# A recurrent layer with low-rank weights padded to full tiles, and VectorE's first scans moved ahead of the group sum

## The reference, cut to what matters

```python
xa = _ln(x, ln1_w, ln1_b)
sx = concatenate([state[:, 1:2] - xa[:, :1], xa[:, :-1] - xa[:, 1:]], axis=1)
xxx = tanh((xa + sx * maa_x) @ maa_w1).reshape(b, l, 5, DM)          # DM = 32
xxx = einsum('blfd,fde->blfe', xxx, maa_w2)
xm = xa[:, :, None] + sx[:, :, None] * (maa_stack + xxx)
xk, xw, xv, xr, xg = (xm[:, :, j] for j in range(5))
w = exp(-exp(time_decay + tanh(xw @ td_w1) @ td_w2))                 # td_w1: 256 x 64
r, k, v = xr @ Wr.T, xk @ Wk.T, xv @ Wv.T;  g = silu(xg @ Wg.T)
def step(s, rkvw):                                                   # along the sequence
    a = k_t[..., :, None] * v_t[..., None, :]
    out = einsum('bhi,bhij->bhj', r_t, u * a + s)
    return a + w_t[..., :, None] * s, out
og = group_norm(out) * gn_w + gn_b                                   # per head of 8
x1 = x + og * g @ Wo.T
# then a second row norm and a small feed-forward, added to x1
```

## Time and profile before

| | us |
|---|---|
| median of three runs | 963.16 (961.91 to 963.85) |
| profiled execution | 962.38 |
| its span, first to last instruction | 960.6 |
| TensorE busy | 918.6 (96%) |
| VectorE busy | 591.4 (62%) |
| ScalarE busy | 462.9 (48%) |
| GpSimd busy | 413.3 (43%) |

### The profile page before, as it was taken

The page is one execution under the profiler, slowest core; times in us unless marked ns, Lnnn a source line. Parts: engine busy times, 40 slices in busy tenths (PEclk is TensorE's granted clock), DMA queues, the critical chain, the costliest instruction groups (busy, mean ns, idle before and its releaser), DMA issues.

```text
span 960.6 us, 23348 instructions
## 1 busy us (share of the span) xinstructions
PE 918.6 (96%) x9345; PEld 767.8 (80%) x9345; DVE 591.4 (62%) x974; ACT 462.9 (48%) x1026; POOL 413.3 (43%) x572
## 2 busy tenths in 40 slices
PE   6999989988999999999999999999998999899998
PEld 4777767976778889888887888888887888678775
DVE  5899986776654343544356443344436757998883
ACT  3677775237743433333435333333333344566565
POOL 2143345965346443423256443343323952343231
PEclk9999999999999999999999999999999999999999
DMA  9100000410011101112101110111100100000000
GB/s 295 47 23 2 2 1 2 140 56 1 2 56 51 53 26 44 53 51 56 56 8 56 51 56 25 55 40 56 51 24 18 56 1 1 2 1 7 12 7 23
DMA packets 24177, 37.64 MB, mean 39 GB/s; under 512 B 4432, under 2 KB 16528, under 8 KB 23824
## 3 DMA queue, kind: packets, MB, share of 16 engines
q1 hardware_dynamic: 24080, 36.23, 12.2%
HBM read 35.17 MB, written 1.05 MB: 38 GB/s over the span
## 4 chain that ended last, share of the span: by engine, by line
PE 70%; DVE 14%; ACT 6%; POOL 5%; issue 5%; DMA 0%; SPq 0%; DVEq 0%; ACTq 0%; POOLq 0%
PE ps L1299 18%; PE ps L790 13%; PE ps L1316 10%; PE ps L1957 6%; PE ps L1334 4%; PE ps L890 3%; PE ps L1360 3%; PE ps L1344 2%; DVE sb L2485 2%; DVE sb L656 1%; DVE sb L650 1%; PE ps L2035 1%; PE ps L421 1%; PE ps L270 1%; PE ps L2121 1%
## 5 line engine op out<-in xcount | busy, mean ns | idle before, releaser
L837 POOL TENSOR_TENSOR sb<-sb 128x256 fp32r<-128x256 f32 (+1 forms) x128 | 102.0, 797 | 255.3 <-DMA sb<-in_heads_a 135.3
L1299 PE MATMUL ps<-sb 128*128 128x512 f32 x768 | 188.4, 395 | 1.0 <-issue 1.0
L1299 PEld LDWEIGHTS ps<-sb 128*128 128x128 f32 x768 | 139.5, 188 | 33.7 <-issue 6.1
L790 PE MATMUL ps<-sb 128*128 128x256 f32 x1152 | 148.8, 286 | 0.2 <-DVE sb L936 0.2
L790 PEld LDWEIGHTS ps<-sb 128*128 128x128 f32 x1152 | 141.5, 191 | 2.6 <-issue 0.6
L839 POOL TENSOR_TENSOR sb<-sb 128x256 fp32r<-128x256 f32 (+1 forms) x128 | 118.4, 925 | 10.0
L1511 DVE TENSOR_REDUCE sb<-ps 128x8 f32<-128x520 f32 x32 | 22.4, 700 | 126.3 <-PE ps L1334 126.3
L1316 PE MATMUL ps<-sb 128*128 128x256 f32 x768 | 99.1, 285 | 0.4 <-DVE sb L1499 0.4
L1316 PEld LDWEIGHTS ps<-sb 128*128 128x128 f32 x768 | 95.0, 191 | 3.0 <-issue 0.9
L1434 ACT ACTIVATE sb<-ps,sb 128x512 f32<-128x512 f32 x64 | 43.8, 685 | 107.4 <-PE ps L1299 107.4
L1531 DVE SCALAR_TENSOR_TENSOR sb<-ps,sb 128x512 fp32r<-128x512 f32 x64 | 45.1, 746 | 72.1 <-ACT sb L1467 72.1
(11 more groups left out here) (221 smaller groups left out, 1674.5 us busy)
## 6 DMA issues: line engine op xcount, KB each, us to landing
sb<-in_heads_a SPq DMA_DIRECT2D x32, 386.0 KB, 3.1
sb<-in_heads_c SPq DMA_DIRECT2D x16, 256.0 KB, 3.8
sb<-in_heads_b SPq DMA_DIRECT2D x32, 128.0 KB, 3.2
sb<-in_mlp_a SPq DMA_DIRECT2D x16, 128.5 KB, 2.0
sb<-in_mlp_b SPq DMA_DIRECT2D x16, 128.0 KB, 2.1
sb<-in_w_r SPq DMA_DIRECT2D x1, 2048.0 KB, 7.6
sb<-in_encT SPq DMA_DIRECT2D x1, 1024.0 KB, 6.4
sb<-in_ctx SPq DMA_DIRECT2D x1, 1024.0 KB, 8.3
```

The lines of the kernel that those rows point to most:

```text
L790: last = pe.matmul(m.acc(t), lhsT[x], rhs[w], start=opens and n == 0, stop=False, skip_group_check=True)
L837: pool.tensor_tensor(high, src, one, ALU.mult).then_inc(*G.did(name + "_high", u))
L1299: last = pe.matmul(m.ps[u][:, c, :], m.w_parts[u][w][:, (KD * q + k) * P:(KD * q + k + 1) * P], rows[x][:, k, c * 512:(c + 1) * 512], star ...
```

## The change

Two things are changed. The low-rank weights are padded with zeros: the lora weight from five blocks of 64 columns to six, so that its third product has 128 columns too; the first decay weight from 64 to 128 columns and the second from 64 to 128 rows, with ScalarE's tanh between them over 128 partitions. And in VectorE's slot `scan0` is called behind `products1` and ahead of `group_sum`, where it stood behind `lora_rows` before; in the drain the two are swapped in the same way.

```diff
--- before.py
+++ after.py
@@ -36,7 +36,7 @@
 HS = 8
 DM, ND = 32, 5
 DD = 64
-NX = 5 * 64
+NX = 6 * 64
 
 COLS = [("ln1_s", 2), ("ln1_b", 2), ("bq_self", 2), ("bk_self", 2), ("bv_self", 2), ("ln2_s", 2), ("ln2_b", 2),
         ("bq_cross", 2), ("bk_cross", 2), ("bv_cross", 2), ("ln3_s", 2), ("ln3_b", 2),
@@ -1978,10 +1978,9 @@
         pe.wait_ge(*m.own_vec.at("xl", i))
         if i >= 1:
             pe.wait_ge(*done["mixed"].at(i - 1))
-        for n, width in enumerate((P, P, 2 * DM)):
-            cols = slice(n * P, n * P + width)
-            last = product(m.mx_ps[0:width, n * P:(n + 1) * P],
-                           [(m.maa_w1[:, k, cols], m.xl[i % 2][:, k, :]) for k in range(KD)])
+        for n in range(NX // P):
+            cols = slice(n * P, (n + 1) * P)
+            last = product(m.mx_ps[:, cols], [(m.maa_w1[:, k, cols], m.xl[i % 2][:, k, :]) for k in range(KD)])
         last.then_inc(*done["lora"].did(i))
 
     @of_tile
@@ -2004,7 +2003,7 @@
             pe.wait_ge(m.s_acc, 16)
         if i >= 1:
             pe.wait_ge(*done["ew"].at(i - 1))
-        product(m.td_ps[0:DD, 0:P], [(m.td_w1[:, k, :], mixed(i, MIX_W, k)) for k in range(KD)])\
+        product(m.td_ps[:, 0:P], [(m.td_w1[:, k, :], mixed(i, MIX_W, k)) for k in range(KD)])\
             .then_inc(*done["td1"].did(i))
 
     @of_tile
@@ -2226,7 +2225,7 @@
         act.wait_ge(*done["td1"].at(i))
         if i >= 1:
             act.wait_ge(*done["td2"].at(i - 1))
-        act.activation(m.td[:, :], m.td_ps[0:DD, 0:P], ACT.Tanh).then_inc(*done["td"].did(i))
+        act.activation(m.td[:, :], m.td_ps[:, 0:P], ACT.Tanh).then_inc(*done["td"].did(i))
 
     @of_tile
     def gate(i):
@@ -2572,12 +2571,12 @@
             vec.wait_ge(m.s_biased, 5)
             add_half(vec, m, 1)
         products1(slot - 5)
+        scan0(slot - 5)
         group_sum(slot - 6)
         shift(slot - 3)
         lora_rows(slot - 3)
         if slot == 3:
             mlp_split(vec, ph, m, 1, 1, 3)
-        scan0(slot - 5)
         group_rstd(slot - 6)
         group_norm(slot - 6)
         scan1(slot - 5)
@@ -2594,8 +2593,8 @@
     bonus(LAST - 1)
     out_heads(LAST - 1)
     products1(LAST)
+    scan0(LAST)
     group_sum(LAST - 1)
-    scan0(LAST)
     group_rstd(LAST - 1)
     group_norm(LAST - 1)
     scan1(LAST)
@@ -2735,13 +2734,13 @@
             {"self": sb([P, S])[:, :], "cross": sb([P, TILES * S])[:, :]} for _ in range(2))
 
         m.s0 = m.mask_mul["cross"][:, 0:TILES * HS * 4].rearrange("p (t n) -> p t n", t=TILES)
-        m.td_w2 = m.mask_mul["cross"][0:DD, TILES * HS * 4:TILES * HS * 4 + D]
+        m.td_w2 = m.mask_mul["cross"][:, TILES * HS * 4:TILES * HS * 4 + D]
         for masks in (m.mask_mul, m.mask_add):
             masks["cross"] = masks["cross"].rearrange("p (t s) -> p t s", s=S)
 
         m.maa_w1, m.maa_w2 = sb([P, KD, NX]), sb([P, 3, D])
         m.sel, m.gather, m.center = sb([P, 2, P]), sb([P, 2, 32]), sb([P, P])
-        m.td_w1 = sb([P, KD, DD])
+        m.td_w1 = sb([P, KD, P])
         m.vj = 3
 
         m.wa, m.wb = pair([P, PACK_A]), pair([P, D])
@@ -2827,7 +2826,7 @@
         m.av, m.sc = cut(0, at, [HS, 4, S]), cut(0, at, [HS, D])
         m.th, m.ew = cut(0, at, [D]), cut(0, at, [D])
         at = [rest]
-        m.td, m.og, m.sq, m.tok, m.yT = cut(1, at, [P], DD), cut(1, at, [D]), cut(1, at, [D]), cut(1, at, [D]), cut(1, at, [KD, P])
+        m.td, m.og, m.sq, m.tok, m.yT = cut(1, at, [P]), cut(1, at, [D]), cut(1, at, [D]), cut(1, at, [D]), cut(1, at, [KD, P])
         m.xc = cut(1, at, [KD, 2, S + 1])
         m.kr, m.kk, m.thf, m.rf = (cut(1, at, [D]) for _ in range(4))
 
@@ -3057,8 +3056,8 @@
     p, n = np.arange(P)[:, None], np.arange(P)[None, :]
     same = p // HS == n // HS
     turned = n % 16 == p // HS
-    w1 = np.zeros((KD, P, ND, 2 * DM), np.float32)
-    w1[:, :, :, 0:DM] = L3("maa_w1").reshape(KD, P, ND, DM)
+    w1 = np.zeros((KD, P, NX // (2 * DM), 2 * DM), np.float32)
+    w1[:, :, 0:ND, 0:DM] = L3("maa_w1").reshape(KD, P, ND, DM)
     w2 = np.zeros((2, 2 * DM, 3, D), np.float32)
     for f in range(ND):
         w2[f % 2, 0:DM, f // 2], w2[f % 2, DM, f // 2] = L3("maa_w2")[f], L3("maa_stack").reshape(ND, D)[f]
@@ -3078,7 +3077,8 @@
         "w_qkv": block(L0("w_qkv")), "w_ao": block(L0("w_ao")), "w_q": block(L0("w_q")), "w_kv": block(L0("w_kv")),
         "w_co": block(L0("w_co")),
         "w1x1": np.ascontiguousarray(np.stack([L1(n) for n in ("Wn", "Wm", "Wl", "Wo")]).transpose(2, 0, 1)),
-        "maa_w2": w2.reshape(P, 3, D), "maa_w1": w1.reshape(KD, P, NX).transpose(1, 0, 2), "td_w1": block(L3("td_w1")), "td_w2": L3("td_w2"),
+        "maa_w2": w2.reshape(P, 3, D), "maa_w1": w1.reshape(KD, P, NX).transpose(1, 0, 2), "td_w1": np.pad(block(L3("td_w1")), ((0, 0), (0, 0), (0, P - DD))),
+        "td_w2": np.pad(L3("td_w2"), ((0, P - DD), (0, 0))),
         "w_r": np.ascontiguousarray(np.stack(stack).transpose(2, 0, 1).reshape(KD, P, 8, D).transpose(1, 2, 0, 3)),
         "s0": np.ascontiguousarray(ctx[:, 2:2 + HS, :].reshape(TILES, 2, KD, P, HS).transpose(3, 0, 4, 2, 1)
                                    [:, :, values].reshape(P, TILES, HS * 4)),
```

## The result

| | before | after |
|---|---|---|
| median, us | 961.92 (14 runs, 959.25 to 963.85) | 966.51 (14 runs, 963.38 to 967.39) |
| ratio, 95% interval | | 1.0047 (1.0037 to 1.0057) |
| span of the profiled execution | 960.6 | 965.3 |

The change makes the kernel 0.47% slower. 963.8 was forecast, and the result lies above the range. The forecast added 0.6 us to the 963.16 of three runs; against the 961.92 of fourteen the change costs 4.6 us.

The account below looks back on a forecast made before the run. VectorE was taken to bound the first stretch, TensorE the second, a chain of latencies the drain. Terms -0.2 + 1.0 + 1.4 - 2.2 + 0.6 = +0.6 on 963.16 gave 963.8 us; range 960.3 to 966.2.

Parts of the forecast that it names:

- second stretch: 850.3 to 923.9 us, TensorE sets the pace: padding saves 0.61 a round for three rounds, 0.33 in the fourth; -2.2 us.
- 0.18 of cover: In later rounds, TensorE's 18.14 us was to stay longer than VectorE's 17.96, so that TensorE sets the round.
- Entry: Start of the layer: first two lora products save 0.25 and 0.14, scans cost +0.29, shorter first stall -0.1; net -0.2 us.
- First stretch: 803.4 to 850.3 us, VectorE sets the pace: late group norm costs +1.0 us in its first round, +1.4 in the second.
- Drain: Last tiles at the layer's end: later group sum delays the root and GpSimd's gate product; +0.6 us.
- the slower one: Rival: VectorE becomes the bound in later rounds, 18.7 us or more each; +2.8 us, 966.0; chance 0.22.
- The faster one: Rival: VectorE's shift does not stand behind GpSimd's operation, so both stalls go; -3.7 us, 959.5; chance 0.23.
- the padding saves nothing: Rival: wider weight loads show between TensorE's passes; +0.4 us at the layer's start, 2.2 not regained, 966.4; chance 0.08.

## Why the prediction was wrong

The step that failed is the second stretch, and in it the sentence that the saving "needs a TensorE round of 18.14 to be the longest, against VectorE's 17.96: 0.18 of cover". Both sums were right to 0.1: TensorE's is 18.14 with the padding alone, and VectorE's is 18.93 - 0.88 = 18.05 in the changed kernel. But the longest of two engines' sums is not the round. The loop over both is a third candidate, and it is longer than either. The rows for it were there: before, `turn_ffn` came 0.95 behind `ffn`'s end, of which some 0.15 is the hand-over (889.14 to 889.29 after), so 0.80 was in hand. From `mix1` to `ffn` VectorE grew from 13.93 to 15.10, by 1.17, and the padded TensorE reaches `turn_ffn` 0.42 sooner after `mix1` (868.44 to 883.32 with the padding alone, 14.88; 870.28 to 885.58 before, 15.30). 1.17 + 0.42 - 0.80 = 0.79, the 18.93 less 18.14 that was measured. With the growth of 0.87 that the prediction itself had for VectorE, the loop would have come out at 18.63, and most of the saving would have been gone. By size, the second stretch is 2.75 us of the 4.1 by which the change in span (4.7) differs from the forecast (0.6), the first stretch 0.96 and the drain 0.35.

Term by term:
- **Entry**, -0.2: -0.16 at the second `mix2`, and -0.03 at the bonus product behind the first round's scans (820.32 against 820.35), where the forecast has its -0.2. In this run the layer itself begins 0.28 later (its first `shift` at 786.46 against 786.18), so the change's own gain is 0.31 there. The term was right to about 0.1.
- **First stretch**, +1.0 and +1.4: +3.36. The mechanism was right, the size was not: the shift takes 1.95 (about 1.9 forecast), the turn of the heads waits 1.73 (1.5 forecast). Each round lacked the scans' wait of 0.31 for the product ahead of them, which group sum, shift and lora rows had hidden; with it the turn of the heads is 1.53 + 0.31 = 1.84 late, which is what the trace has (829.40 against 827.56). The -0.2 that the sum took over from the entry was not there, as just said. The sum itself, 1.53 - 0.2 - 0.45, makes 0.88 and not 0.83; nothing hangs on that.
- **Second stretch**, -2.2: +0.55. The 1.17 are the shift's stall (+1.53), the first of the five scans that no longer stands (-1.15), the scans' wait (+0.31) and the last scan beside GpSimd's gate product (+0.46), together 1.15. The stall and the gate product were in the forecast for VectorE's sum; the wait was not, and none of them was set against `ffn`. Of the -2.2, 0.33 was for the fourth round, which lies in the last piece. It does not come even with the padding alone (46.23 against 46.24): there TensorE waited for `ffn` already before.

```profile
921.91 0.41 PE L2098 MATMUL ps<-sb 128*128 128x128 f32 x2 [0.60 <-DVE sb L2546]
```

- **Drain**, +0.6: +0.95. The wait for GpSimd is 1.20, as forecast; the scans' wait of 0.31 is about the rest by size, but that was not tried by itself.

Of the rivals, the slower one named the right stretch and nearly the right time (966.0), but not the cause: VectorE kept 0.88 of idle time a round, and with `ffn` earlier the same work fits into 18.14. The faster one is refuted by the shift itself. That the padding saves nothing is refuted by the padding alone, at 0.61 a round.

By the Trainium skill (TensorE: Matmul & The Clock Gate, LDWEIGHTS) a load takes its time by its columns, so the wider loads, with nothing hidden, would have given back some of the saving. Here they gave back nothing: the 0.61 is what the prediction had worked out without them, and TensorE's passes fill 54.43 of 54.43 while the loads are busy for 45.52 of the same time. The Trainium skill (SBUF — State Buffer, Who interferes with whom) has VectorE contend with a GpSimd operation that reads SBUF when it has two inputs in SBUF itself, and never in a reduction. The trace agrees: beside GpSimd's 1.81 the two-input shift took 1.95, the group sum 0.39.

## What to carry to other kernels

Where a stretch is near balance between two engines, the longest engine sum is not enough: follow each buffer that one engine hands back to the other, and add up the whole way round. An instruction that waits with time in hand shows how far such a loop is from setting the pace; subtract from that both what the waited-for engine loses and what the waiting one gains. An edit that shortens the waiting engine's way to the wait spends the same slack as one that delays the other, and what it saves past that is lost: here the padding is worth 0.61 a round with the old order and 0.18 with the new one.

An instruction between a result and its first reader can hide the hand-over, even on one and the same engine (here 0.31 a round). Before it is moved away, ask what it covered.

## What the runs showed of the hardware that was not expected

- VectorE can wait for its own results: 0.23 us of idle time between the 1.20 us product and the scans that read it, in every round but the first where the scans stand right behind it. With the group sum between them there is none of it, and the group sum itself starts 1.12 behind the product's start, the scans alone 1.43. Not every such hand-over costs as much: the sum behind the bonus product (L2511), which reads what that has just written, starts 0.04 behind its end (820.32 and 0.41, then 820.77). In the source five semaphore waits stand ahead of the scans and one ahead of that sum; whether that makes the difference, no run shows.
- GpSimd's multiply cost VectorE much the same wherever two-input work from SBUF stood beside it: 1.53 at the shift, 1.2 at a scan when norm and reciprocal cover its beginning, 1.45 in the lora rows, 1.6 in the scans when it comes late. The orders tried here moved it and did not remove it.
- A wait of 0.60 on TensorE costs 0.76 of its time from start to start. From the products ahead of `turn_ffn` to `turn_ffn` it is 2.96 in the change (886.33 to 889.29), and 2.20 with the padding alone (881.12 to 883.32), where it does not wait and starts 0.17 before these products' 2.37 have ended.
